# Where the neighbour gathers and maxima of a graph network stand in a software-pipelined order

## What is computed

```
x = x + relu(concat(xn, max over first 25 neighbours of xn) @ W + b)   # xn = layernorm(x)
x = x + top2_of_8_experts(layernorm(x))      # gelu(x @ W1[e] + b1[e]) @ W2[e] + b2[e]
x = x + masked_attention(layernorm(x), adj)  # 8 heads of 16
x = x + top2_of_6_experts(layernorm(x))      # three small layers each
```

## Time and profile before

| | us |
|---|---|
| median of three runs | 3596.99 |
| range of the three | 3594.17 to 3603.11 |
| the profiled execution | 3601.75 |
| its span, first to last instruction | 3599.6 |

### The profile page before, as it was taken

One profiled execution on the slowest core, in us unless ns is written; L12 is line 12 of the kernel. 1 busy time (PEld: TensorE's weight loads), 2 busy tenths in 40 slices (PEclk: granted clock), 3 DMA queues, 4 the chain that ended last, 5 costly groups with the idle time before them and its releaser, 6 DMA issues.

```text
span 3599.6 us, 46254 instructions
## 1 busy us (share of the span) xinstructions
PE 2146.0 (60%) x14209; PEld 1346.9 (37%) x14209; DVE 1776.8 (49%) x5239; ACT 1226.7 (34%) x2295; POOL 1106.3 (31%) x1215
## 2 busy tenths in 40 slices
PE   0010332057847775686748684677658778785687
PEld 0010231044425532454435442454345435442344
DVE  4134127167626663666446662566446436525713
ACT  2001122024623353235513462235423443362153
POOL 3536455431642144303540254313440110100000
PEclk9985675577968887797959896788869888897898
DMA  4323754662474236623564247523663044203000
GB/s 114 39 45 72 139 120 105 95 150 85 92 130 110 92 69 91 155 91 71 98 129 122 66 85 124 112 84 70 102 134 109 21 74 151 75 24 53 25 7 7
DMA packets 190672, 318.14 MB, mean 88 GB/s; under 512 B 28975, under 2 KB 115244, under 8 KB 190380
## 3 DMA queue, kind: packets, MB, share of 16 engines
q1 hardware_dynamic: 156844, 245.99, 24.3%
q0 software_dynamic: 33536, 68.75, 16.5%
HBM read 271.31 MB, written 42.93 MB: 87 GB/s over the span
## 4 chain that ended last, share of the span: by engine, by line
issue 35%; DVE 27%; PE 26%; DVEq 5%; ACT 4%; DMA 2%; SPq 1%; ACTq 0%
DVE parts L1221 7%; PE PA L1579 4%; PE PA L1582 4%; PE PY L1594 4%; ACT HB L1375 2%; PE PH L1529 2%; DVEq L861 2%; DVE res_f L1115 2%; PE PA L1556 2%; PE PY L1541 2%; DVE score L909 1%; DVE top L913 1%; PE PH L1636 1%; DMA rows_cols<-sorted_x 1%; DVE st L870 1%
## 5 line engine op out<-in xcount | busy, mean ns | idle before, releaser
L1221 DVE CUSTOM_DVE_ANT_0 parts<-PA,mask 128x1024 bf16<-128x1024 f32 x512 | 625.5, 1222 | 291.6 <-issue 291.6
L803 POOL DMA_INDIRECT G<-table,slot_idx x512 | 526.7, 1029 | 270.2 <-issue 270.2
L1375 ACT ACTIVATE HB<-PA 128x1024 f32<-128x1024 f32 x512 | 498.9, 1020 | 323.4 <-PE PA L1582 321.2
L1556 PE MATMUL PA<-KS,QS 96*128 96x512 bf16 x1024 | 356.2, 441 | 261.5 <-DVE res_f L1115 141.5
L1579 PE MATMUL PA<-QS,KS 99*128 99x512 bf16 x1024 | 420.6, 411 | 102.2 <-ACT HB L1375 69.9
L636 POOL TENSOR_TENSOR pool_pad<-pool_pad 1x1 f32<-1x1 f32 x146 | 29.1, 200 | 1462.0 <-DMA sorted_y<-rows_y 743.2
L1582 PE MATMUL PA<-identb,mask 128*128 128x128 bf16 x4096 | 423.8, 229 | 0.0
L639 DVE MEMSET dve_pad<- 1x1 f32 x699 | 41.1, 59 | 751.9 <-DMA G_more<-table,slot_idx 434.5
L1582 PEld LDWEIGHTS PA<-identb,mask 128*128 128x128 bf16 x4096 | 338.8, 103 | 141.1 <-issue 31.5
L803 POOL DMA_INDIRECT G_more<-table,slot_idx x280 | 287.1, 1025 | 173.4 <-issue 173.4
L1358 ACT ACTIVATE HB<-PH,block_b 128x128 f32<-128x128 f32 x736 | 209.6, 368 | 353.7 <-PE PH L1529 353.6
(11 more groups left out here) (218 smaller groups left out, 3291.1 us busy)
## 6 DMA issues: line engine op xcount, KB each, us to landing
wbuf<-in_L_ffn_W SPq DMA_DIRECT2D x128, 512.0 KB, 4.2
adj_sb<-in_adj SPq DMA_DIRECT2D x64, 512.0 KB
adjm<-in_adj SPq DMA_DIRECT2D x64, 512.0 KB
HB<-in_L_ffn_W SPq DMA_DIRECT2D x32, 512.0 KB, 3.6
parts<-in_L_ffn_W SPq DMA_DIRECT2D x24, 512.0 KB, 4.8
parts_dram<-parts SPq DMA_DIRECT2D x16, 768.0 KB, 4.0
QS<-parts_dram SPq DMA_DIRECT2D x48, 256.0 KB, 9.3
KS<-parts_dram SPq DMA_DIRECT2D x48, 256.0 KB, 19.5
```

The costliest lines, as they stand in the source:

```text
L803: pool.indirect_dma_start(G[:, t % 2, s, :] if s < few else G_more[:, s - few, :], None, table, bass.IndirectOffsetOnAxis(slot_idx[:, t, s ...
L1221: ins = dve.tensor_tensor_reduce(out=junk, in0=psum(ps, step)[:, :], in1=mask[:, t, :], scale=1.0, scalar=LOWEST, op0=ALU.add, op1=ALU.max ...
L1375: act.activation(HB[:, kc % 2, 2 * pr:2 * pr + 2, :], psum(ps, key)[:, :].rearrange("p (h q) -> p h q", h=2), ACT.Exp, scale=float(D) ** - ...
L1556: ins = pe.matmul(psum(ps, step)[:, half[hf]], QS[0:SROWS, h, t * P:(t + 1) * P], KS[0:SROWS, h, half[hf]], start=True, stop=True)
```

## The change

`FETCHED` goes from 4 to 2, so `POOLED` from 3 to 1. The value part keeps the gathers of tiles 0 and 1 and the maximum of tile 0. Gathers of tiles 2 and 3 and maxima of tiles 1 and 2 go to the next pass's score part, ahead of the others. In the score part maxima now come every 16 units from 1 on (before every 15 from 0); in the value part the gathers are due at 30 and 65 (before 30, 45, 60, 75), and tile 0's maximum at 105 (before 82).

```diff
-FETCHED = 4
+FETCHED = 2
 POOLED = FETCHED - 1
...
     if near:
-        streams.append([(15.0 * (t - POOLED), ("pmax", t), (("fetch", t),)) for t in range(POOLED, TILES)])
-        streams.append([(15.0 * (t - POOLED) - 14.0, ("fetch", t), (("pmax", t - 1),)) for t in range(FETCHED, TILES)])
+        streams.append([(16.0 * (t - POOLED) + 1.0, ("pmax", t), (("fetch", t),)) for t in range(POOLED, TILES)])
+        streams.append([(16.0 * (t - POOLED) - 14.0, ("fetch", t), (("pmax", t - 1),)) for t in range(FETCHED, TILES)])
...
-        streams.append([(30.0 + 15.0 * t, ("fetch", t), (("find", t), ("store_x",), ("pmax", t - 1)))
+        streams.append([(30.0 + 35.0 * t, ("fetch", t), (("find", t), ("store_x",), ("pmax", t - 1)))
                         for t in range(FETCHED)])
-        streams.append([(82.0 + 17.0 * t, ("pmax", t), (("fetch", t),)) for t in range(POOLED)])
+        streams.append([(105.0 + 17.0 * t, ("pmax", t), (("fetch", t),)) for t in range(POOLED)])
```

## The result

| | before | after | ratio, 95% interval |
|---|---|---|---|
| median, us | 3595.58 (4 runs, 3586.60 to 3603.11) | 3499.92 (4 runs, 3495.44 to 3504.68) | 0.9735 (0.9707 to 0.9764) |
| profiled execution, us | 3601.75 | 3495.44 | |
| its span, us | 3599.6 | 3493.7 | |

The forecast was 3503 in a range of 3430 to 3560, so the time is 3 us from it. The terms behind it were not all as near; the two traces show where the 105.9 us of span went. (The medians differ by 95.7 us; the two profiled executions lie on opposite sides of theirs, so some 10 us of the 105.9 are spread between executions.) "Gap" is from here on the time from V's copy (L1334) to the first score maximum (L1221), and "value part" the time from the last score maximum to V's copy.

The account below looks back on a forecast made before the run. VectorE's waits for gathers were taken to delay the last copy and first score at ends of passes 4 to 8. Gaps -115, score parts +52, passes 1 to 4 -31 sum to -94 us: 3597 to 3503, range 3430 to 3560.

Parts of the forecast that it names:

- The gap: V's copy to first score, ends of passes 4 to 8: 38.6 us each, 193 together instead of 307.9, so -115 us.
- pass 9's 30.6 us: V's copy to first score at pass 9's end, where no gathers run; claimed as what each gap can shrink to.
- the 8 us for gathers and loads: Added to each gap for gathers and the residual's load on the same DMA engines; 8 us, bounds 0 and 13.7.
- the most that can go there: Lateness of the last `av` copy at ends of passes 4 to 8: 34.9, 35.1, 36.2, 18.2, 18.3 us, 143 together.
- The score part: First to last score, passes 5 to 9: two more maxima and tile 2's wait lengthen it by 52 us together.
- The price of a maximum: Each eight-slot maximum added among the scores costs 4.3 us, against 2.9 us of its instructions.
- Tile 2's wait: VectorE waits for tile 2's gathers after the fourth score in passes 5 to 7: 5 to 12 us, taken as 8.
- Passes 1 to 4: Gather chain of passes 1 to 3 unchanged (0, within 10 us); pass 4's last score at 817 to 825, -31 us.
- The value part: Last score to V's copy: no change in length forecast; growth there was named as a sign of being wrong.
- More gain: Rival: gathers fill holes (-34), tile 2 lands early (-24), added maxima cost 2.9 us (-14); 3431 us, chance 0.15.
- Less gain: Rival: tile 2 waits 16 us instead of 8 (+24), transfers lose 12 instead of 8 (+20); 3547 us, chance 0.18.
- Slower: Rival: tile 2's gather chain bounds each score part, 24 us wait, transfers delayed, pass 4 loses 20; 3621 us, chance 0.06.

Follow-up runs that it names:

- A: Chip of the main result: changed kernel against the kernel before, 3499.92 against 3595.58 us, ratio 0.9735.
- D: Second chip with short value parts: changed kernel against the kernel before, 3506.86 against 3597.96 us, ratio 0.9751.
- the kernel before with the copy: Kernel before plus an unused 2 MB device-memory copy issued by SyncE behind QS and KS; 3922.54 us, ratio 1.0082 to before.
- the three late tiles: Changed kernel with FETCHED = 3: gathers due at 30, 65, 85, maxima at 97 and 113 in the value part; 3556.51 us, ratio 0.9883 to before.

## Why the prediction was right

**The gap: right as a sum, its mechanism right at three ends of five.** The forecast was 193 us for five, and A shows 193.2, D 191.5. The last copy is on time, tile 1's maximum is late for nothing, and the way from V's copy to the first score is pass 9's 30.6 us of the earlier trace rows and what gathers and loads add: 37.1 to 39.8. That the 8 us for gathers and loads came out to the us is luck: they were chosen between 0 and 13.7, the 1.3 us in them for the residual's load stand on no row, and no run separates them. What kept the first score waiting was not always the late copy. At the ends of passes 4 to 6 it was 35 us late and 20.4 to 24.5 us went. At the ends of passes 7 and 8 it was 18 us late, "the most that can go there", but 26.0 and 20.2 us went. There VectorE waited 20.19 us and 20.88 us for tile 3's second eight ahead of the first score, and the kernel before with the copy has gaps of 55 and 57 us with the last copy on time. The prediction read that wait but counted it only in the score part. Its sum was right all the same, since it was taken from pass 9's end and not from the lateness. The 12.14 us at the loop's branch (below) were not in the sum and did no harm: VectorE still waits 8.04 us for TensorE ahead of the first score, and the gaps with the branch (39.8, 39.4, 37.4 us) are as long as those without (37.1, 39.5).

**The score part: right in sign, two terms off in opposite directions.** +52 was forecast; D has +50.6, A +40.3. The price of a maximum was too high: with the sum's own 150.0 us for a pass without any and 1.3 us for a second eight, and with the measured waits, 3.2 us a maximum are left on A and 3.3 on D, not 4.3, which is 30 to 34 us over thirty. The waits were too low: 45.9 us on A and 48.1 on D over the five score parts, where the sum had 24. So the nearness on D is partly luck. Tile 2's wait was 8 us in the sum and 12.30 to 12.41 on A in passes 5 to 7, just above the stated 5 to 12. The sum put its landing at 1448 to 1455, after a first score at 1435, that is 13 to 20 us behind it, and it came at 20.4 (1407.36 less 1386.93). Its first eight were issued from 1371.22 on, 16 us ahead of the first score where the sum had 20; the pause before the second eight was 7.89 us, within the 5 to 10 of the sum. Passes 8 and 9 took 181.1 and 170.2 us on A, for 178.4 and 177.1. That tile 3 costs no wait there was right but for 1.41 us; that tile 5 of pass 8 would wait (7.41 on A, 12.32 on D) was not foreseen.

**Passes 1 to 4: right.** The gather chain of passes 1 to 3 stayed (the product with `agg` of pass 3 is 4.2 us earlier on A, 0.8 on D), and the last score of pass 4 is at 813.9 and 814.7 us, a little before the 817 to 825 of the forecast. Tiles 1 and 2 land at 662.8 and 695.2, where the sum had 664 and 696 to 702.

**The value part: not foreseen.** It was named as what would make the prediction wrong, and it grew by 8.2 and 8.5 us over five, all of it in passes 7 and 8 (164.0 and 163.9 us on A, 164.0 and 164.8 on D). The two parts of both traces show the same place: TensorE idles 1.63 to 1.68 us for `wts`, its granted clock falls from 1.00 to 0.50 for some 10 us, and each part ends 6 us later. In passes 7 and 8 of before, and in those of the three late tiles, the same idle time is 1.31 to 1.46 us and the clock stays at 1.00. So the 6 us are the clock's; what made it fall in one kernel and not in the other no run varied.

**The rivals.** More gain (3431) had three parts. The gathers fill holes and tile 2 lands early: neither happened. Added maxima at little more than their bare 2.9 us: that is what the traces show. Less gain (3547) had a tile 2 wait of 16 us and 12 us lost by the transfers; they were 12.4 and 8.0. Slower (3621) needed a tile 2 wait of 24 us by its sum; it was 12.4. What decides it is visible in the three late tiles, where such a chain does stand ahead of the score and takes back 50 us of 91. A gather into `G` on GpSimd in after's score part of pass 6, with two more maxima in it, takes a median of 997 ns and 1222 at most; in before it was 999 and 1410. The lockout that the Trainium skill (SBUF — State Buffer, Who interferes with whom) describes for descriptor writes does not show, so by these rows the prediction was right to keep it out of the sum. It is no test of that rule: the section names VectorE's two-port modes as its cause and says that `tensor_tensor`, of which the maxima consist, has none.

## What to carry to other kernels

When an engine's in-order queue waits for a chain of gather batches ahead of work that another engine needs, move that wait behind the needed work; a step that is merely late matters much less (15 us of lateness cost 2 to 8 us here, a wait for the chain some 20 us). Price each moved step by the engine that bounds the place it moves to: among the scores VectorE is the bound, and a step cost about its own length. Measure on more than one chip before a few per cent are believed: the same change was worth 2.65% and 2.5% on two chips and 1.9% on a third, through other terms of the sum.

## What the hardware showed that was not expected

- **The loop's branch under full DMA engines.** At the end of pass 5 VectorE stood idle 12.14 us with no release in the profile ahead of its first instruction of the next turn (1365.47); in before it was 4.42 us at the same place (1443.37), with the QS and KS transfers over by then. In the run of three late tiles it was 6.14 us. The idle time is long where the branch comes soon behind the start of these transfers; what the engine waits for the profile does not name, and no run tested it.
- **Two groups of chips.** Before took 3596 and 3598 us on two chips and 3869 to 3894 on three. The traces on the three have value parts of 208 to 225 us instead of 158, with stalls of all engines but GpSimd. The score parts differ little.
- **2 MB of traffic costs 6 to 7 us of a gap whose DMA engines are already full** (203.2 to 238.6 us over five). Alone they would be 10 us at the 207 GB/s of that stretch, so it seems that a part of them went into what the others left; this is an estimate.
- **A wait of 1.6 us and 10 us at half clock.** In the value parts of passes 7 and 8 of after TensorE idled 1.63 to 1.68 us, and its granted clock fell to 0.50. The same matmuls (L1464) then took 3.78 us instead of 1.98. In before the idle time at that place was 1.31 to 1.46 us and the clock stayed at 1.00.
